# Self attention in quads of heads: column-tiled value products, late division

## What is computed

```python
Q = rope(proj(Wq, bq)); K = rope(proj(Wk, bk)); V = proj(Wv, bv)      # 32 heads of 16
scores = jnp.einsum('bhqd,bhkd->bhqk', Q, K) / math.sqrt(D_HEAD)
scores = jnp.where(causal[None, None], scores, jnp.float32(-jnp.inf))
attn = jax.nn.softmax(scores, axis=-1)
out = jnp.einsum('bhqk,bhkd->bhqd', attn, V)
return out.transpose(0, 2, 1, 3).reshape(B, S, N_HEADS * D_HEAD) @ Wo.T + bo
...
x = _layernorm(x + self_attention(x))
x = _layernorm(x + cross_attention(x, ctx))
x = _layernorm(x + ffn(x))
```

## Time and profile before

| | us |
|---|---|
| median of 3 runs | 2960.67 (2955.37 to 2963.62) |
| the profiled execution | 2956.6 |
| its span, first to last instruction | 2954.8 |
| TensorE busy | 2760.3 (93% of the span) |
| DVE, ACT, POOL busy | 2100.3, 1973.2, 1660.6 |
| mean granted TensorE clock | 0.979 |

### The profile page before, as it was taken

One profiled execution on the slowest core, in us unless ns is written; L12 is line 12 of the kernel. 1 busy time (PEld: TensorE's weight loads), 2 busy tenths in 40 slices (PEclk: granted clock), 3 DMA queues, 4 the chain that ended last, 5 costly groups with the idle time before them and its releaser, 6 DMA issues.

```text
span 2954.8 us, 60508 instructions
## 1 busy us (share of the span) xinstructions
PE 2760.3 (93%) x20272; PEld 2576.1 (87%) x20272; DVE 2100.3 (71%) x4364; ACT 1973.2 (67%) x4392; POOL 1660.6 (56%) x1663
## 2 busy tenths in 40 slices
PE   7899999998899999999899999999988999999996
PEld 6789999998679999999768999999967899999995
DVE  5477777778557878787755877777766587878785
ACT  4476676767457777677655877777756576767673
POOL 4288897947115656565611656555552265656564
PEclk9999999999899999999999999999989999999998
DMA  5446464612311212121331112121232121212112
GB/s 186 139 165 216 160 231 158 211 58 101 119 48 44 94 51 94 51 94 51 122 102 44 63 67 76 69 74 71 78 119 86 42 74 57 89 55 90 55 55 100
DMA packets 97921, 285.10 MB, mean 96 GB/s; under 512 B 9936, under 2 KB 18256, under 8 KB 94416
## 3 DMA queue, kind: packets, MB, share of 16 engines
q1 hardware_dynamic: 97616, 281.24, 27.3%
HBM read 237.16 MB, written 44.04 MB: 95 GB/s over the span
## 4 chain that ended last, share of the span: by engine, by line
PE 67%; issue 11%; POOL 9%; ACT 5%; DVE 5%; DMA 2%; DVEq 0%; ACTq 0%; SPq 0%; POOLq 0%
PE bank L1030 39%; PE dn L1030 14%; PE sp L1030 9%; POOL kept_s L527 4%; ACT ph L714 2%; PE sp L1161 1%; POOL orw L546 1%; PE sp L1169 1%; POOL ol L550 1%; ACT pn L641 1%; PE sp L1101 1%; PE sp L1248 1%; DVE mcol L909 1%; POOL hib L517 1%; ACT sp L719 1%
## 5 line engine op out<-in xcount | busy, mean ns | idle before, releaser
L527 POOL TENSOR_TENSOR kept_s<-kept_s,mrow 128x512 f32<-128x512 f32 (+1 forms) x896 | 1062.3, 1215 | 596.8 <-ACT mrow L704 596.7
L920 DVE TENSOR_TENSOR pl<-sp,ph 128x512 fp32r<-128x512 f32 (+1 forms) x896 | 576.9, 644 | 79.3 <-ACT sp L719 75.8
L714 ACT ACTIVATE ph<-kept_s 128x512 fp32r<-128x512 f32 (+1 forms) x896 | 534.1, 596 | 45.7 <-POOL kept_s L527 42.8
L719 ACT ACTIVATE sp<-kept_s 128x512 f32<-128x512 f32 (+1 forms) x896 | 506.1, 565 | 2.1 <-DVE sua L928 2.1
L1030 PE MATMUL dn<-ph,vh 128*128 128x256 f32 (+1 forms) x1664 | 489.4, 294 | 2.2 <-DVE pl L920 1.7
L1030 PE MATMUL dn<-ph,vl 128*128 128x256 f32 (+1 forms) x1664 | 471.4, 283 | 0.0
L1030 PE MATMUL dn<-pl,vh 128*128 128x256 f32 (+1 forms) x1664 | 470.7, 283 | 0.0
L928 DVE TENSOR_TENSOR sua<-sp,sua 128x512 f32<-128x512 f32 (+1 forms) x640 | 400.2, 625 | 0.0
L696 ACT ACTIVATE kept_s<-bank 128x512 f32<-128x512 f32 x384 | 228.5, 595 | 232.0 <-PE bank L1030 231.4
L696 ACT ACTIVATE kept_s<-sp 128x512 f32<-128x512 f32 x384 | 228.6, 595 | 193.0 <-PE sp L1030 192.6
L1030 PEld LDWEIGHTS dn<-ph,vh 128*128 128x128 f32 (+1 forms) x1664 | 316.5, 190 | 10.3 <-DVE pl L920 3.4
(11 more groups left out here) (149 smaller groups left out, 6967.4 us busy)
## 6 DMA issues: line engine op xcount, KB each, us to landing
wqx<-wq SPq DMA_DIRECT2D x128, 512.0 KB, 3.3
wox<-wo SPq DMA_DIRECT2D x64, 1024.0 KB, 4.8
wk<-wk SPq DMA_DIRECT2D x32, 512.0 KB, 3.3
wvx<-wv SPq DMA_DIRECT2D x16, 1024.0 KB, 5.6
raw<-in_ctx_t SPq DMA_DIRECT2D x48, 200.0 KB, 2.4
wqk<-in_ws SPq DMA_DIRECT2D x17, 513.0 KB, 4.0
raw<-in_wq_in SPq DMA_DIRECT2D x32, 256.0 KB, 3.8
wq<-hib SPq DMA_DIRECT2D x32, 256.0 KB, 2.0
```

The source lines that it names most:

```text
L527: nc.gpsimd.tensor_tensor(kept_s[:, n % 2, i:z, :], kept_s[:, n % 2, i:z, :], mrow[:, n % 2, :].unsqueeze(1).broadcast_to([P, z - i, S]), ...
L714: nc.scalar.activation(ph[:, k % PH, 0:cols], src, ACT.Exp, scale=XSCALE).then_inc(ph_ok, 1)
L719: nc.scalar.activation(pbank[k % 2][:, 0:cols], src, ACT.Exp, scale=XSCALE).then_inc(pr_ok, 1)
L920: nc.vector.tensor_tensor(pl[:, k % PH, 0:cols], src, ph[:, k % PH, 0:cols], ALU.subtract).then_inc(pl_ok, 1)
```

## The change

The heads go in quads (`u` counts 8 quads of a sequence, `j` the head in it, `QH4 = 4`).

- The score banks are the four banks of `sp4`, one quad deep. `score_quad(u)` waits for all eight exponentials of the quad before.
- The exponentials lose `accum_out`. DVE no longer forms row sums' reciprocals per head, nor multiplies `pn`. The undivided exponentials are transposed and copied to `pt`, which is now one quad deep (`pn` is eight heads deep).
- `weigh_quad` takes the value products of four heads together: each head has a stationary tile of 32 columns and writes its own 32 PSUM partitions of `dn` (four column tiles). The same is done with `oe`, a tile of ones, into `s_den`, which gives the row sums. `take_turned` waits until the quad before has been weighed.
- Once per group DVE takes the reciprocal of `s_den` (128x256) and multiplies `dn` by it (`divide_heads`); `take_heads` then adds the bias.
- The orders on TensorE, ACT and DVE are written anew; SP's is as before. `take_v` has four small copies in place of two. POOL clears a `vx` of 1024 columns in place of 4608, and fills `oe`.

```diff
-        pj, s_bank, s_turn = bank[0], [bank[1][:, :], bank[2][:, :], mx[:, 0, :], mx[:, 1, :], pv[:, 0, :]], pv[:, 1, :]
+        pj, s_bank, s_turn, s_den = bank[0], [sp4[:, j, :] for j in range(QH4)], bank[1], bank[2]
...
+                def quad_exps(u, j):
+                    n = (b * NQ + u) * QH4 + j
+                    act.wait_ge(s_mx, 2 * (n + 1))
+                    if n >= PNR:
+                        act.wait_ge(s_tp, n - PNR + 1)
+                    for qb, (a, z) in enumerate(((0, P), (P, 3 * P))):
+                        nc.scalar.activation(pn[:, n % PNR, a:z], s_bank[j][:, a:z], ACT.Exp,
+                                             bias=nmx[:, n % PNR, qb:qb + 1]).then_inc(s_exp, 1)
+                def take_turned(u, j):
+                    n = (b * NQ + u) * QH4 + j
+                    act.wait_ge(s_tp, n + 1)
+                    if b * NQ + u:
+                        act.wait_ge(s_pvq, b * NQ + u)
+                    nc.scalar.activation(pt[:, j, :], s_turn[:, 0:3 * P], ACT.Copy).then_inc(s_ptc, 1)
...
-                for g in range(NSH + 2):
...
+                for u in range(NQ + 1):
+                    m, e = divmod(u, 2)
+                    for j in range(QH4):
+                        if u:
+                            take_turned(u - 1, j)
+                        if u < NQ:
+                            quad_exps(u, j)
+                        if e and m and j == 1:
+                            take_heads(m - 1)
+                        if m + 1 < NM and e == 0 and j == 2:
+                            take_qk(m + 1)
+                        if m + 1 < NM and e and j == 3:
+                            take_v(m + 1)
+                        if u < NQ and j % 2:
...
+                            high_part(ctxh[:, mc, a:z], raw[:, r % 2, 0:z - a])
...
+                def divide_heads(m):
+                    t = b * NM + m
+                    dve.wait_ge(s_pvq, 2 * (t + 1))
+                    nc.vector.reciprocal(rcs[:, :], s_den[:, 0:S]).then_inc(s_fin, 1)
+                    dve.wait_ge(s_fin, 2 * t + 1)
+                    dve.wait_ge(s_ot, at(t, 1, 0))
+                    nc.vector.tensor_tensor(otn[:, :], dn[:, 0:S], rcs[:, :], ALU.mult).then_inc(s_fin, 1)
...
+                for u in range(NQ):
+                    m, e = divmod(u, 2)
+                    if e and m:
+                        divide_heads(m - 1)
+                    for j in range(QH4):
+                        quad_maxima(u, j)
...
+                divide_heads(NM - 1)
...
+                def turn_head(u, j):
+                    n = (b * NQ + u) * QH4 + j
+                    pe.wait_ge(s_exp, 2 * (n + 1))
+                    pe.wait_ge(s_ptc, n)
...
+                def weigh_quad(u):
+                    t, e = b * NM + u // 2, u % 2
+                    pe.wait_ge(s_ptc, (b * NQ + u + 1) * QH4)
+                    pe.wait_ge(s_v, 4 * (t + 1))
+                    if e == 0:
+                        pe.wait_ge(s_fin, 2 * t)
+                    for kb, a, z, w in ((0, 0, 0, S), (1, S, P, P)):
+                        for part in range(2):
+                            for j in range(QH4):
+                                out_rows, i = slice(32 * j, 32 * (j + 1)), e * QH4 + j
+                                last = mm((s_den if part else dn)[out_rows, z:z + w], oe[:, e, :] if part else vx[:, t % 2, kb, i, :],
+                                          pt[:, j, a:a + w], e == 0 and kb == 0, e == 1 and kb == 1)
+                    last.then_inc(s_pvq, 1)
...
+                for u in range(NQ + 1):
+                    m, e = divmod(u, 2)
+                    if u:
+                        turn_head(u - 1, 0)
+                    if u < NQ:
+                        score_quad(u)
+                    for j in range(QH4):
+                        if u and j:
+                            turn_head(u - 1, j)
+                        if m + 1 < NM:
+                            if e == 0 and j < 2:
+                                project_qk(m + 1, j)
+                            elif e and j == 0:
+                                swap_pairs(m + 1)
+                            elif e and j == 2:
+                                project_v(m + 1)
+                    if u:
+                        weigh_quad(u - 1)
```

More of the change, by code:

```diff
@@ L167, in raw_of_weight @@
     return NM * len(SA_RAW) + k - NM * SA_W
[L170 to L178, removed]
+NQ = 2 * NM
+QH4 = HB // 2
+PNR = 2 * QH4
 def late_first(rows):
@@ L501, in _, with clear_values @@
             pool.sem_inc(ot_ok, 1)
-            nc.gpsimd.memset(vx[:, :, :, :], 0.0).then_inc(s_vz, 1)
+            def clear_values():
+                nc.gpsimd.memset(vx[:, :, :, :, :], 0.0).then_inc(s_vz, 1)
+                nc.gpsimd.memset(oe[:, :, :], 0.0).then_inc(s_vz, 1)
+                pool.wait_ge(s_vz, s_vz_at[0] + 2)
+                for e in range(2):
+                    nc.gpsimd.memset(oe[:, e, e * DH:(e + 1) * DH], 1.0).then_inc(s_vz, 1)
+                s_vz_at[0] += N_VZ
+            clear_values()
             def ctx_low_part(b, m, k, r):
@@ L616, in take_v @@
                     act.wait_ge(s_vp, at(t, 1, 1))
-                    if t:
-                        act.wait_ge(s_pv, at(t, HB, -HB))
+                    if t >= 2:
+                        act.wait_ge(s_pvq, 2 * (t - 1))
                     for tb in range(TB):
-                        nc.scalar.activation(vx[:, t % 2, tb, :].rearrange("p (h x) -> p h x", h=HB)[:, :, 0:DH],
-                                             pj[:, tb * P:(tb + 1) * P].rearrange("p (h x) -> p h x", h=HB),
-                                             ACT.Copy).then_inc(s_v, 1)
+                        for e in range(2):
+                            nc.scalar.activation(vx[:, t % 2, tb, e * QH4:(e + 1) * QH4, e * DH:(e + 1) * DH],
+                                                 pj[:, tb * P:(tb + 1) * P].rearrange("p (j e d) -> p e j d", e=2, d=DH)[:, e],
+                                                 ACT.Copy).then_inc(s_v, 1)
@@ L631, in _ @@
                 take_qk(0)
                 take_v(0)
-                for g in range(NSH + 2):
[L634 to L649, removed]
-                    if i == 3 and m + 1 < NM:
-                        take_qk(m + 1)
-                    if i == 7 and m + 1 < NM:
-                        take_v(m + 1)
-                    if i in (1, 3, 5, 7) and m < NM:
-                        k = i // 2
-                        r = raw_at(b, m, 2 * k if b == 0 else k)
-                        a, z = CTX_PIECES[k]
-                        act.wait_ge(raw_ld[r % 2], 16 * (r // 2 + 1))
-                        high_part(ctxh[:, m, a:z], raw[:, r % 2, 0:z - a])
```

140 lines of the change are left out of this document (54 added, 86 removed).

## The result

The changed kernel takes **3000.31 us** (median of 4 runs, 2996.66 to 3005.38); the kernel before, measured beside it, 2962.14 (4 runs, 2955.37 to 2965.03). The ratio is 1.0133, with a 95% interval of 1.0110 to 1.0157: slower by about 38 us, where +19 was forecast (2980, in a stated range of 2945 to 3015). The profiled execution took 2996.66 us, with a span of 2994.6.

A forecast was written before the change was run, and what follows sets the result against it. TensorE was taken as nearly the bound of the self attention stages, with hand-overs making them longer. +13 us (three like stages) and +6 (first) gave +19: 2976 on the profiled execution, 2980 on the median, range 2945 to 3015.

The forecast's parts named there:

- ladder of hand-overs: Self attention stages: quad-by-quad sum of TensorE, ACT and DVE prices and waits; each like stage +4.4 us, three times +13.
- Even quads: Like stages: an even quad with projections takes 10.3 us, TensorE waiting 0.8 before turn 3, 1.3 before the block; odd 8.8.
- both stands for `wqk`: First sequence: TensorE stands 6.0 us for `wqk` behind quad 2's masks, and 4 more behind quad 4's masks.
- The end, quad 7 to output projection: Stage end: four turns and copies one by one, 1.14 us each; output projection at 15.8 against 11.05, +4.8.
- the reciprocal of 128x256, "some 0.4 us": DVE's division once per group: priced like other operations per column, 0.4 us, also the lower end; upper end 2.3.
- the rival's mechanism: Slow reciprocal: 1.9 us more at each division, 4.9 per like stage, 2 in the first; 2997 us; chance 0.24.
- A reciprocal over 1 us: DVE's division: one of the signs named in advance that would show the prediction wrong.
- the block, 1.85: TensorE's products per quad: 1.85 us, twice the row-tiled score quad's 0.87 plus 0.1; lower end 1.30, upper 5.2.
- The first sequence, +6: First self attention stage: output projection at 111.4 against 106.50, +5, with the load chain's lateness taken as +6 us.
- Faster, TensorE is the bound: Rival: hand-overs overlap, so stages shrink with TensorE's work, -6.0 each, three times -18; 2943 us; chance 0.13.
- A cheap block brings it back to zero: Whole kernel: cheap block, together with the own case's low edge, leaves time within 0.3% of before; chance 0.17.
- No tiles side by side: Rival: column tiles run one after another, block 5.2 us, 3.3 more; +80 in three stages; 3080 us; chance 0.07.

The follow-up runs named there:

- e1: Changed kernel with the 128x256 reciprocal replaced by a copy of the same shape, leaving the division out: 2981.99 us, 1.0087 of the kernel before.
- e2: Changed kernel with the next group's query and key projections moved behind turns 1 and 2 of the quad: 2969.5 us (one run).
- e3: Changed kernel with row sums in the free half of `dn`'s bank and two banks for turned heads: 2976.47 us, 1.0068 of the kernel before.
- e4: Changed kernel with unused matmuls where TensorE would stand (larger dose), row sums in `dn`'s bank: 2980.0 us, 1.0085 of the kernel before.
- e5: Changed kernel with later projections, row sums in `dn`'s bank and two banks for turned heads: 2959.61 us, 1.0014 of the kernel before.
- e8: Changed kernel with fewer unused matmuls where TensorE would stand, row sums in `dn`'s bank: 2974.83 us, 1.0060 of the kernel before.
- e12: Changed kernel with only the load of `wqk` for group m+2 issued earlier on SP: 2994.25 us, 1.0124 of the kernel before.

## Why the prediction was right in sign and too small

**Right.** The stages alone are longer; +19 was worked out by a ladder of hand-overs, and the ladder holds while the clock is full. In the second sequence of the changed kernel the score quads start 0.0, 7.08, 15.56, 26.07, 35.37, 45.19, 54.02 and 62.86 us after the first. Quad 0 to 2: 15.56, forecast 15.4. Even quads 10.5 and 9.8, forecast 10.3; odd 9.3 and 8.8, forecast 8.8. Some of this agreement is luck: the block was 0.41 us cheaper than forecast, and ahead of odd quads' maxima the reciprocal cost about as much again (8.8 against 8.5 in e1); the even quad of 10.5 has a stretch at the lower clock in it, the one of 9.8 has not. The last quad's turns each stand behind a copy, and both stands for `wqk` came, the first 6.42 us for 6.0, the second 3.71 for 4. That the order and the single turn bank make the ladder, e2 and e3 show by taking its parts away.

**Failed: the clock has no term.** The prediction took every TensorE price at the 1.00 of the earlier trace rows and read the new stands (0.8, 1.3, 0.64 per turn at the end) as their own length alone. They also brought the clock down to its lower level in parts of each stage, and the prices of that stretch are then 1.5 to 1.9 times those used: turn 0.87 for 0.5, block 2.72 for 1.85. "The end, quad 7 to output projection" was 15.8 and measured 20.1, 21.6 and 20.1 us, 14.4 over in three stages; quads 0 to 7 measured 62.9, 63.7 and 63.0 for 61.5, together 5.0 over. Not all of the end's 14.4 is the clock's: with the copy for the reciprocal (e1) the three ends take 5.2 us less in sum (18.15 for 20.08 in the fourth sequence). e4, with the slow reciprocal and the clock near full, has ends of 17.6, 19.2 and 17.6, 7.3 less in sum. e5, with fewer stands, comes to 16.5. In all, filling the stands took 14 us off the four stages (e4, e8) and the copy 6.7 (e1), of the 29 by which the stages exceeded the forecast; no run separates the rest.

**Failed: the reciprocal of 128x256, "some 0.4 us".** It measured 1.76, within the stated bounds of 0.4 and 2.3 but near the other end: the rival's mechanism with 1.36 for its 1.9 us. A reciprocal over 1 us had been named as a sign of being wrong. The two-column row could not tell: 0.95 us at 128 columns and 1.76 at 256 give, as an estimate, 6.3 ns per column and 0.14 us besides, so two columns are some 13 of that row's 154 ns; that it "is no dearer than its like" was no evidence. That the rival's 2997 lies within 4 us of the measured 3000.3 is luck: it gave the reciprocal 16.7 us, and leaving it out took 6.7 off the stages.
**Failed, in the other direction: the block, 1.85.** It measured 1.44 at full clock, close to the streaming bound of 1.30. I had scaled four row tiles, 0.87 for 384 columns; column tiles come cheaper than that. By the prediction's arithmetic 8 x 0.41 = 3.3 us a stage less; but a block that runs wholly at the lower clock takes 2.72, and three of the third stage's eight do (those at 1579.40, 1590.03 and 1598.87), which gives back 3.8 there.

**Failed: the first sequence, +6.** +15.5 measured. The two stands cost 10.1 as said, and e12 removes 10.2. The rest is the prices of the other stages again: quad 6 took 9.5 us for 7.9 and the end 21.7 for 15.8. And this stage has the lowest clock of all, 0.84:

```profile
20.00:40.00 20.00, 15.75 (x153) 12.13 (x152) 11.42 (x30) 12.16 (x37) 9.50 (x10) 0.97 0.49 160
40.00:52.00 12.00, 6.04 (x23) 4.88 (x24) 0.79 (x3) 2.29 (x7) 1.42 (x3) 0.72 0.38 128
```

Behind the long stand the clock is down for one projection, which costs 3.38 us (45.28 to 48.66) where the prediction has 1.79; then it is full again:

```profile
45.00:49.00 4.00, 3.72 (x12) 3.02 (x13) 0.00 (x0) 0.00 (x0) 0.00 (x0) 0.57 0.03 10
49.00:52.00 3.00, 2.33 (x14) 1.87 (x13) 0.00 (x0) 2.29 (x7) 1.20 (x2) 1.00 0.01 3
```

The second stand's projection costs 3.24, so both together some 3 us more.

**The sum.** Like stages 247.7 us for the 228 forecast, +19.6; the first 96.8 for 87.3, +9.5; the rest of the program -8.7, which no term held and which is luck. Together 20.4 of the 20.7 us by which the profiled execution missed 2976. "Faster, TensorE is the bound" fell clearly: in the second sequence TensorE is 3 us less busy even at its lower clock, and stands 13 us more (81.7 - 60.8 against 71.6 - 63.7). "A cheap block brings it back to zero" had the block right and the result wrong. "No tiles side by side" is excluded by 1.44 us.

## What to carry to other kernels

A TensorE that is freed of work but must wait for each hand-over can pay twice, for the stand and for the slower clock behind it: when a change turns busy time into many short stands, work the ladder out at both clock levels and take the two sums as bounds. Which stretch falls to the lower level I cannot forecast from these runs: the last quad's turns ran at the lower in the third sequence, and three of four at the higher in the second and fourth. Before merging many small steps into a late wide one, ask what runs beside it at the end of the stage, and take the price of a wide reciprocal from a wide one. Keep two banks for a result that goes back and forth, and put independent work into the stand, not ahead of the step that starts the chain.

## What the hardware showed unexpectedly

- A reciprocal on DVE takes 154 ns at 128x2, 0.95 us at 128x128 and 1.76 us at 128x256, where a copy of 128x256 takes 0.425.
- Four f32 column tiles of 32 columns stream side by side almost without loss: 768 columns per tile, two passes each, in 1.44 us, against 0.65 us for 384 columns on the whole array.
- TensorE's granted clock fell to 0.86 to 0.89 on the mean in stages of 82 to 84 us in which it was busy for 61 to 64 and stood at most 2.9 us at a time. Useless matmuls in the stands (TensorE busy for 66 to 71) kept it at 0.96 to 1.00 and made these stages 2 to 4 us shorter.
- The output projection behind the end of the third stage takes 8.84 us in the changed kernel; in the first sequence before it took 7.14, as it does in e4's third: the slower clock reaches into the work behind the stands.
